# Cross-attention and quantised FFN on one core: an eight-batch loop written out, its small jobs regrouped, and maxima reduced pair by pair

## The chip, the cores and the metric

One core of a Trainium2 chip runs the whole layer for all eight batches. The metric is the device time of one execution in microseconds (us), lower is better. Times of the kernel before and after are medians of several executions.

## The reference

For each of 8 batches `x` is 512 rows by 256 and the context is 1601 rows by 256; there are 16 heads of 16 columns, all float32.

```
x   = x + attention(layernorm(x), ctx, ctx)      # 16 heads of 16, softmax over 1601 keys
h   = silu(fp4(layernorm(x)) @ fp4(Wg).T) * (fp4(layernorm(x)) @ fp4(Wu).T)
out = x + fp4(h) @ fp4(Wd).T                     # hidden width 704
fp4(v): v in blocks of 16, scaled by max|v|/6, rounded to the FP4 grid, scaled back
```

## The kernel before

**Steps.** Attention of a batch takes 52 steps: 4 groups of 4 heads, and in each group 13 tiles of the context (124 or 123 rows each, `KROWS`). A step n does this, in this order on each engine:

- TensorE (PE): `scores(n, 0)`, two score matmuls (head pair 0) into the two `st` banks; the shared jobs of side 0; `scores(n, 1)`, head pair 1 into the same two banks, each of which must first have been read by the exponential of pair 0; two "pair products" into `mx` (score rows against 512 keys, from which the softmax maximum comes); `weighted(n - 1)`, the four probability times value products of the step before into `pvb`; the shared jobs of side 1.
- ScalarE (ACT): `exps(n, 0)`, two exponentials; its share of side 0; `exps(n, 1)`; at the start of a group the copy of `pvb`; its share of side 1.
- VectorE (DVE): its share of side 0; the maxima of the step's products; its share of side 1; then the "extras" (layer norm, scales, rounding).
- GpSimd (POOL) splits queries and keys into three bf16 parts and does rounding; it has a table by step as well.

**Three batches at once.** While batch i is in attention ("att"), the same 52 steps carry the preparation of batch i + 1 ("early": context and x transposed, `q`, `k`, `v` projections) and the FFN of batch i - 1 ("late": `pvT`, `attT`, `o`, `xqT`, `gate`, `up`, `hqT`, `down`). These jobs all go through one PSUM bank, `misc`, one after the other. The dictionary `SLOTS` says which job stands in which step and on which side; each job is followed by the engine that takes its result out of `misc`. ACT takes `ctxT`, `xnT`, `q`, `k`, `v`, `attT`, `xqT`, `hqT`, `wT` and the tanh of `gate`; DVE takes `nm`, `pvT`, `o`, `gate`, `up`, `down`.

**Order of the whole.** `iterations` runs the body as pre (early work of batch 0 alone, same 52 slots), first (att of batch 0, with the FFN weights quantised and transposed, `wT`, "once"), a hardware loop `Fori(0, 6)` of six batches, last, and tail (FFN of batch 7 alone).

**Maxima.** They run 18 steps ahead of attention (`M_LEAD`). A step makes two products, one in each half of `mx`; where both are full, `maximum_of_two` reduces both (128x2048) with one DVE instruction, which frees both halves at its end.

**Queue of SyncE (SP).** It issues loads and stores in program order. In pre: context, x, then queries and keys to DRAM and back (`queries_out`, `queries_in`, `keys_out`, `keys_in`). In first, `raw_in` (FFN weights) stands right behind the next batch's context load. The context is loaded as `ctx_rows[0:123, 2:13]` from a source whose outermost dimension is those 123 rows. The projection weights come over ACT's queue at the very start.

Of the kernel before, what the change touches and what calls it, by code (L numbers as in the profile page):

```python
# [6 lines left out]
I32 = mybir.dt.int32  # L7
ALU = mybir.AluOpType
# [4 lines left out]
I = 704  # L13
NC2 = E // 128
QT = S // 128
NKT = 13
KROWS = [124, 124] + [123] * 11
# [36 lines left out]
M_LEAD = 18  # L54
BIAS_AT = STEPS - M_LEAD - 1
# [6 lines left out]

SLOTS = {
    0: ([("v", 5, "att")], []),
    1: ([("v", 6, "att")], [("pvT", 3, "late")]),
    2: ([("attT", 0, "late")], [("attT", 1, "late")]),
    3: ([("o", 0, "late")], []),
    4: ([("o", 1, "late")], []),
    5: ([("ctxT", 0, "early")], []),
    6: ([("ctxT", 1, "early")], [("ctxT", 2, "early")]),  # L70
    7: ([("ctxT", 3, "early")], [("ctxT", 4, "early")]),
    8: ([("ctxT", 5, "early")], [("nm", 1, "att")]),
    9: ([("ctxT", 6, "early")], [("xnT", 0, "early")]),
    10: ([("xnT", 1, "early")], []),
    11: ([("q", 0, "early")], [("wT", 0, "once")]),
    12: ([("k", 0, "early")], [("wT", 1, "once")]),
    13: ([("k", 1, "early")], [("wT", 2, "once")]),
    14: ([("k", 2, "early")], [("pvT", 0, "att")]),
    15: ([("k", 3, "early")], [("wT", 3, "once")]),
    17: ([("q", 1, "early")], []),  # L80
    18: ([("xqT", 0, "late")], [("xqT", 1, "late")]),
    19: ([("gate", 0, "late")], []),
    20: ([("gate", 1, "late")], [("wT", 4, "once")]),
    21: ([("k", 4, "early")], [("nm", 2, "att")]),
    22: ([("gate", 2, "late")], [("wT", 5, "once")]),
    23: ([("gate", 3, "late")], []),
    24: ([("k", 5, "early")], [("wT", 6, "once")]),
    25: ([("gate", 4, "late")], [("wT", 7, "once")]),
    26: ([("gate", 5, "late")], []),
    27: ([("k", 6, "early")], [("pvT", 1, "att")]),  # L90
    28: ([("gate", 6, "late")], []),
    29: ([("gate", 7, "late")], []),
    30: ([("k", 7, "early")], [("wT", 8, "once")]),
    31: ([("up", 0, "late")], [("wT", 9, "once")]),
    32: ([("up", 1, "late")], []),
    33: ([("up", 2, "late")], []),
    34: ([("up", 3, "late")], [("nm", 3, "att")]),
    35: ([("up", 4, "late")], [("wT", 10, "once")]),
    36: ([("up", 5, "late")], [("wT", 11, "once")]),
    37: ([("up", 6, "late")], []),  # L100
    38: ([("up", 7, "late")], []),
    39: ([("hqT", 0, "late")], [("hqT", 1, "late")]),
    40: ([("down", 0, "late")], [("pvT", 2, "att")]),
    41: ([("hqT", 2, "late")], []),
    42: ([("v", 0, "early")], [("hqT", 3, "late")]),
    43: ([("down", 1, "late")], []),
    44: ([("v", 1, "early")], [("hqT", 4, "late")]),
    45: ([("hqT", 5, "late")], []),
    46: ([("v", 2, "early")], []),
    47: ([("down", 2, "late")], [("nm", 0, "early")]),  # L110
    48: ([("v", 3, "early")], [("hqT", 6, "late")]),
    49: ([("hqT", 7, "late")], []),
    50: ([("down", 3, "late")], []),
    51: ([("v", 4, "early")], []),
# [3 lines left out]
    1: ([], [("pvT", 3, "late")]), 2: ([("attT", 0, "late")], [("attT", 1, "late")]), 3: ([("o", 0, "late"), ("o", 1, "late")], []),  # L118
# [12 lines left out]
def slots(kind, n):  # L131
    return (TAIL_SLOTS if kind == "tail" else SLOTS).get(n, ([], []))
# [3 lines left out]
for _step in SLOTS.values():  # L136
# [5 lines left out]
    1: [("early", "stats", 0)], 2: [("early", "stats", 1), ("early", "mean", 0)], 3: [("early", "root", 0)],  # L142
    4: [("early", "apply", 0)], 5: [("late", "stats", 0), ("early", "apply", 1)],
    6: [("late", "stats", 1)], 7: [("late", "mean", 0)], 9: [("late", "root", 0)],
    10: [("late", "apply", 0), ("late", "apply", 1)], 11: [("late", "xmax", 0)], 12: [("late", "xscale", 0)],
    13: [("late", "xpower", 0)], 17: [("late", "xlast", 0)],
    33: [("late", "hscale", 0)], 35: [("late", "hpower", 0)], 36: [("late", "hscale", 1)], 38: [("late", "hpower", 1)],
    39: [("late", "hscale", 2)], 41: [("late", "hpower", 2)], 42: [("late", "hscale", 3)], 44: [("late", "hpower", 3)],
}
TAIL_EXTRA = {  # L150
    5: DVE_EXTRA[5][:1], **{n: DVE_EXTRA[n] for n in (6, 7, 9, 10, 11, 12, 13, 17)},
    19: [("late", "hscale", 0)], 20: [("late", "hpower", 0), ("late", "hscale", 1)], 21: [("late", "hpower", 1), ("late", "hscale", 2)],
    22: [("late", "hpower", 2), ("late", "hscale", 3)], 23: [("late", "hpower", 3)],
}
# [12 lines left out]
class Iteration:
# [8 lines left out]
    def count(self, part, per, k):  # L176

        n = (self.ahead + SHIFT[part]) * per + k
        if isinstance(self.i, int):
            return self.i * per + n  # L180
        assert n > 0
        return self.i * per + n
# [23 lines left out]
def xattn_ffn(nc, x, ctx_in, wqT, wkT, wvT, woT, bq, bk, bv, bo, w_gate, w_up, w_down, out, scr_k, scr_q):  # L206
    es = ExitStack()
    with es:
# [58 lines left out]
        s_const, s_ones, s_w, s_x, s_x1 = (sem(n) for n in ("s_const", "s_ones", "s_w", "s_x", "s_x1"))  # L267
        s_ctx = [sem("s_ctx0"), sem("s_ctx1")]
# [15 lines left out]
        tanh_done, hs_ready, hy_ready, hm_ready, h_step, hq_ready = (sem(n) for n in ("tanh_done", "hs_ready", "hy_ready", "hm_ready", "h_step", "hq_ready"))  # L284
# [27 lines left out]
        def maxima(it, n):  # L312

            part, first = ("early", 2 * (n - STEPS + M_LEAD)) if n >= STEPS - M_LEAD else ("att", 2 * (n + M_LEAD))
            if part not in it.parts:
                return []
# [25 lines left out]
        def _(sp):  # L342
# [774 lines left out]
```

## Time and profile before

| what | value |
|---|---|
| time, median of 3 executions | 2022.91 us (2022.39 to 2029.71) |
| the profiled execution, its own time | 2027.88 us |
| its span from first to last instruction | 2026.0 us |
| busy share PE, DVE, ACT, POOL | 87%, 67%, 56%, 27% |
| mean granted TensorE clock | 0.957 |

PE is the busiest engine. Its busy time is a modelled one in which neighbouring matmuls overlap, so in this text the cost of a matmul is taken as the distance from its start to the start of what follows it. A step is measured from its first score matmul to the first score matmul of the next step. Seen so, the 2026 us are: pre 127.1, first 246.7, the six batches of the loop 226.7 to 230.5 each, last 200.8, tail 77.9. Inside first, its steps 0 to 4 take 35.2, steps 5 and 6 together 17.2, and step 19 takes 16.7; without a wait such a step is about 3.5. A loop batch without its boundary is 223.7, the same 52 steps as where straight-line code runs into the next batch.

### The profile page before, as it was taken

The numbers are of one execution on the slowest core, as the hardware profiler recorded it, in microseconds if no ns is written. First come the engines' busy times: TensorE is split into PE (matmuls) and PEld (weight loads), VectorE is DVE, ScalarE is ACT, GpSimd is POOL, SyncE is SP. The second block draws the span as 40 slices with busy tenths as digits, with TensorE's granted clock in tenths as the row PEclk, the third lists the DMA queues.
The fourth block names the chain that finished last, engine by engine and source line by source line (L and its number), as shares of the span: only waits on it lengthen the run. The fifth ranks groups of instructions, "written<-read, shape, count | busy, mean of one in ns | idle before, by whom it ended". The sixth has DMA issues, their size and how long they took to land. (4 is left out here: it accounts for less than half of the span.)

```text
span 2026.0 us, 30105 instructions
## 1 busy us (share of the span) xinstructions
PE 1754.9 (87%) x9600; PEld 730.4 (36%) x9600; DVE 1348.5 (67%) x1636; ACT 1127.0 (56%) x2239; POOL 541.8 (27%) x415
## 2 busy tenths in 40 slices
PE   3567688989999899899999899899999899989957
PEld 2222222333343334433343334433344334423425
DVE  1557576776857777676857777576867677576524
ACT  1124466666546665566546665566556665556631
POOL 3203550041320414042320514032320514000414
PEclk9677899999999999999999999999999999999988
DMA  2721431143212332134212322134212422020000
GB/s 66 154 65 27 92 72 33 54 92 65 42 39 52 78 58 40 59 74 79 46 35 52 82 58 38 61 73 71 54 32 49 89 58 39 17 33 1 6 16 11
DMA packets 97768, 109.53 MB, mean 54 GB/s; under 512 B 18484, under 2 KB 83004, under 8 KB 97596
## 3 DMA queue, kind: packets, MB, share of 16 engines
q1 hardware_dynamic: 95500, 106.21, 25.4%
q8 instruction: 89, 1.46, 0.3%
q10 hardware_dynamic: 2096, 1.18, 0.2%
q14 instruction: 83, 0.68, 0.1%
HBM read 76.78 MB, written 30.16 MB: 53 GB/s over the span
## 5 line engine op out<-in xcount | busy, mean ns | idle before, releaser
L763 ACT ACTIVATE prob<-st 123x512 f32<-123x512 f32 (+1 forms) x1664 | 906.9, 601 | 469.1 <-PE st L612 466.9
L811 DVE TENSOR_REDUCE cmx<-mx 128x4 f32<-128x2048 f32 x336 | 769.8, 2291 | 317.6 <-PE mx L626 315.9
L612 PE MATMUL st<-qstack,kstack 112*123 112x512 bf16 (+1 forms) x1664 | 554.6, 401 | 56.3 <-ACT prob L763 29.8
L641 PE MATMUL pvb<-prob,vv 123*17 123x512 f32 (+1 forms) x3328 | 446.2, 609 | 0.0
L612 PEld LDWEIGHTS st<-qstack,kstack 112*123 112x123 bf16 (+1 forms) x1664 | 201.4, 136 | 455.9 <-ACT prob L763 234.6
L626 PE MATMUL mx<-kstack,qstack 48*128 48x512 bf16 (+1 forms) x2048 | 256.6, 343 | 59.7 <-DVE cmx L811 38.1
L575 PE MATMUL misc<-wguT,rowsT 128*128 128x352 f32 x460 | 159.7, 469 | 19.1 <-DVE nmf L845 13.7
L820 DVE TENSOR_REDUCE cmx<-mx 128x2 f32<-128x1024 f32 x96 | 114.9, 1220 | 38.3 <-PE mx L626 38.2
L1021 POOL TENSOR_TENSOR cin<-cin 128x400 f32<-128x400 f32 (+1 forms) x60 | 60.8, 1013 | 284.3 <-ACT cin L716 284.2
L626 PEld LDWEIGHTS mx<-kstack,qstack 48*128 48x128 bf16 x2048 | 57.8, 95 | 216.9 <-issue 133.8
L1021 POOL TENSOR_TENSOR qx<-qx,qp 128x512 f32<-128x512 f32 x16 | 18.5, 1158 | 387.0 <-ACT qp L705 387.0
L641 PEld LDWEIGHTS pvb<-prob,vv 123*17 123x17 f32 (+1 forms) x3328 | 55.4, 95 | 159.8 <-issue 156.7
L538 PE MATMUL misc<-ctxT,wk 128*128 128x400 f32 (+1 forms) x236 | 93.2, 517 | 22.5 <-DVE att L857 12.4
L545 PE MATMUL misc<-wv,ctxT 128*123 128x256 f32 (+1 forms) x392 | 104.8, 413 | 7.1 <-DVE nmf L845 7.1
L575 PEld LDWEIGHTS misc<-wguT,rowsT 128*128 128x128 f32 x460 | 84.9, 191 | 65.8 <-DVE nmf L845 19.1
L1058 POOL TENSOR_TENSOR ht<-ht,mt 128x704 f32<-128x704 f32 x32 | 53.7, 1679 | 184.5 <-DVE mt L939 184.5
L585 PE MATMUL misc<-wdT,hqT 128*128 128x256 f32 x348 | 86.6, 390 | 4.7 <-ACT hqT L742 4.7
L1054 POOL TENSOR_TENSOR ht<-ht,rh 128x704 f32<-128x704 f32 x32 | 44.4, 1386 | 166.7 <-DVE rh L932 165.2
L545 PEld LDWEIGHTS misc<-wv,ctxT 128*123 128x123 f32 (+1 forms) x392 | 78.6, 202 | 27.3 <-DVE nmf L845 10.3
L1034 POOL TENSOR_TENSOR x<-x,bob 128x1024 f32<-128x1024 f32 x8 | 18.7, 2343 | 241.6 <-DMA x<-x 241.6
L867 DVE SCALAR_TENSOR_TENSOR ht<-hqT,misc 128x352 f32<-128x352 f32 x57 | 29.7, 521 | 75.8 <-ACT hqT L730 75.8
L585 PEld LDWEIGHTS misc<-wdT,hqT 128*128 128x128 f32 x348 | 62.4, 189 | 28.0 <-issue 10.7
(169 smaller groups left out, 1546.8 us busy)
## 6 DMA issues: line engine op xcount, KB each, us to landing
kstack<-scr_k SPq DMA_DIRECT2D x384, 100.1 KB, 4.4
scr_k<-cin SPq DMA_DIRECT2D x48, 300.0 KB, 4.3
qstack<-scr_q SPq DMA_DIRECT2D x384, 32.0 KB, 1.9
cin<-ctx_in SPq DMA_DIRECT2D x8, 1353.0 KB
scr_q<-qp SPq DMA_DIRECT2D x16, 384.0 KB, 4.2
scr_k<-cin SPq DMA_DIRECT2D x16, 300.8 KB, 4.5
xn<-x SPq DMA_DIRECT2D x8, 512.0 KB, 6.5
x<-x SPq DMA_DIRECT2D x8, 512.0 KB, 3.6
```

The costliest lines, as they stand in the source:

```text
L538: last = mm(o[:, 0:w], wk[:, h, m * 128:(m + 1) * 128], ctxT[:, h, COFF[n]:COFF[n] + w], start=(h == 0), stop=(h == NC2 - 1))
L545: last = mm(o[0:w, (kt % 2) * E:(kt % 2 + 1) * E], ctxT[:, h, KOFF[kt]:KOFF[kt] + w], wv[:, h, :], start=(kt % 2 == 0 and h == 0), stop=(h ...
L575: last = mm(o[:, 0:IH], rowsT[:, h, t * 128:(t + 1) * 128], wguT[:, h, first:first + IH], start=(h == 0), stop=(h == NC2 - 1))
L585: last = mm(o[:, 0:E], hqT[0:FW[f], f, :], wdT[0:FW[f], f, :], start=(f == 0), stop=(f == NF - 1))
L612: mm(st[0:KROWS[kt], h, :], kstack[:, hd, KOFF[kt]:KOFF[kt] + KROWS[kt]], qstack[:, hd, :], start=True, stop=True).then_inc(st_full, 1)
L626: last = mm(mx[:, q % 2, par, at:at + w], qstack[r0:r0 + LEAD, hd, t * 128:(t + 1) * 128], kstack[r0:r0 + LEAD, hd, k0:k0 + w], start=True ...
L641: last = mm(pvb[32 * h:32 * h + D + 1, :], vv[0:w, kt, HG * g + h, :], prob[0:w, n % 2, h, :], start=(kt == 0), stop=(kt == NKT - 1))
L763: activate(prob[0:KROWS[kt], n % 2, 2 * pair + h, :], st[0:KROWS[kt], h, :], ACT.Exp, scale=SCALE).then_inc(exp_done[2 * pair + h], 1)
L811: v.tensor_reduce(cmx[:, g % 2, h0:h0 + 2, at0:at1 + 1:at1 - at0], mx[:, :, :, :].rearrange("p j h n -> p h j n"), op=ALU.max, axis=AX.X). ...
L820: v.tensor_reduce(cmx[:, g % 2, h0:h0 + 2, at:at + 1], products, op=ALU.max, axis=AX.X).then_inc(max_free, 1)
L1021: g_.tensor_tensor(whole, whole, parts[:, 0, :], ALU.subtract).then_inc(step, 1)
L1058: g_.tensor_tensor(y, y, m, ALU.add).then_inc(h_step, 1)
```

## The change

- `with eng.Fori(0, B - 2)` becomes a Python `for`: the six batches are written out, and all semaphore targets become constants.
- Context tiles have 128 rows (twelve of 128, one of 65), and the context is loaded in three pieces: 2 tiles, 10 tiles, the last 65 rows.
- `SLOTS` is rewritten: the jobs that DVE takes (`nm`, `pvT`, `o`, `gate`, `up`, `down`) and `wT` stand on side 0, and most of those that ACT takes (`q`, `k`, `v`, half of `ctxT` and of `hqT`) on side 1. Some extras move by a step.
- pre has its own table: all seven `ctxT` jobs, then k 0 to 3, then `xnT` and `q`, then k 4 to 7. It does the maxima of group 0 alone (26 products, was 36); the ten others come in the first five steps of first, four products a step in place of two.
- Loads: x before the context; ACT's queue first brings only the weights and biases of `q` and `k`, the others after `ctxT`; the FFN weights (`raw_in`) move from SP's queue to ACT's, the first two pieces at the end of k 4 to 7 in pre, the later ones behind `wT` jobs.
- Tail: the rounding of x (`xround`) goes from POOL to DVE, and of the four hidden blocks DVE rounds 1 and 3 by itself (`hround`) while POOL does 0 and 2.
- `maximum_of_two` is gone: each product of a head pair has its own 128x1024 reduction, which frees its half of `mx`.

```diff
-KROWS = [124, 124] + [123] * 11
+KROWS = [128] * (T // 128) + [T % 128]
...
 SLOTS = {
-    0: ([("v", 5, "att")], []),
-    1: ([("v", 6, "att")], [("pvT", 3, "late")]),
+    0: ([], [("v", 5, "att")]),
+    1: ([("pvT", 3, "late")], [("v", 6, "att")]),
...
-    8: ([("ctxT", 5, "early")], [("nm", 1, "att")]),
-    9: ([("ctxT", 6, "early")], [("xnT", 0, "early")]),
-    10: ([("xnT", 1, "early")], []),
-    11: ([("q", 0, "early")], [("wT", 0, "once")]),
-    12: ([("k", 0, "early")], [("wT", 1, "once")]),
-    13: ([("k", 1, "early")], [("wT", 2, "once")]),
-    14: ([("k", 2, "early")], [("pvT", 0, "att")]),
-    15: ([("k", 3, "early")], [("wT", 3, "once")]),
-    17: ([("q", 1, "early")], []),
-    18: ([("xqT", 0, "late")], [("xqT", 1, "late")]),
-    19: ([("gate", 0, "late")], []),
+    8: ([("nm", 1, "att")], [("xnT", 0, "early")]),
+    9: ([("xnT", 1, "early")], [("q", 0, "early")]),
+    10: ([("wT", 0, "once")], [("k", 0, "early")]),
+    11: ([("wT", 1, "once")], [("k", 1, "early")]),
+    12: ([("wT", 2, "once")], [("k", 2, "early")]),
+    13: ([("wT", 3, "once")], [("k", 3, "early")]),
+    14: ([("pvT", 0, "att")], []),
+    15: ([], [("q", 1, "early")]),
+    17: ([("xqT", 0, "late")], [("xqT", 1, "late")]),
+    18: ([("gate", 0, "late")], []),
...
-    24: ([("k", 5, "early")], [("wT", 6, "once")]),
-    25: ([("gate", 4, "late")], [("wT", 7, "once")]),
+    24: ([("wT", 7, "once")], [("k", 5, "early")]),
+    25: ([("gate", 5, "late")], []),
...
-    50: ([("down", 3, "late")], []),
-    51: ([("v", 4, "early")], []),
+    50: ([], [("v", 3, "early")]),
+    51: ([], [("v", 4, "early")]),
 }
+PRE_SLOTS = {
+    5: ([("ctxT", j, "early") for j in range(7)], []),
+    11: ([("k", j, "early") for j in range(4)], []),
+    14: ([("xnT", j, "early") for j in range(2)], [("q", 0, "early"), ("q", 1, "early")]),
+    15: ([("k", j, "early") for j in range(4, 8)], []),
+    34: ([("v", 0, "early")], []), 36: ([("v", 1, "early")], []), 38: ([("v", 2, "early")], []), 40: ([("v", 3, "early")], []),
+    42: ([("v", 4, "early")], []), 47: ([("nm", 0, "early")], []),
+}
...
-            with eng.Fori(0, B - 2) as i:
+            for i in range(B - 2):
                 body(Iteration("loop", i, 1))
...
+            if it.kind == "first" and n < M_LATE:
+                first, number = M_GROUP + 4 * n, 4
...
-                sp.dma_start(ctx_rows[0:KROWS[0], 0:2, :], ctx_in[bi, 0:n0, :].rearrange("(t p) n -> p t n", t=2)).then_inc(s_ctx[0], 16)
-                sp.dma_start(ctx_rows[0:KROWS[2], 2:NKT, :], ctx_in[bi, n0:T, :].rearrange("(t p) n -> p t n", t=NKT - 2)).then_inc(s_ctx[1], 16)
+                for piece, (t0, t1) in enumerate(((0, 2), (2, NKT - 1))):
+                    sp.dma_start(ctx_rows[:, t0:t1, :], ctx_in[bi, t0 * 128:t1 * 128, :].rearrange("(t p) n -> p t n", p=128)).then_inc(s_ctx[piece], 16)
+                sp.dma_start(ctx_rows[0:KROWS[-1], NKT - 1, :], ctx_in[bi, n1:T, :]).then_inc(s_ctx[2], 16)
...
-                    both = maxima(it, n)
-                    if both and it.kind != "pre" and all(job[5] < M_HEADS - 1 for job in both):
-                        maximum_of_two(*both)
-                    else:
+                    todo = maxima(it, n)
+                    for both in (todo[:2], todo[2:]):
                         for job in both:
                             maximum(job)
...
+TAIL_POOL = {1: POOL_WORK[1], 19: [("late", "hscaled", 0)], 20: [("late", "hround", 0)], 21: [("late", "hscaled", 2)], 22: [("late", "hround", 2)]}
```

## Rows read from the trace of the kernel before

**Rows 1.** Windows of first and of the fourth loop batch: busy us (and instructions) of PE, PEld, DVE, ACT, POOL.

```profile
127.14:373.84 246.70, 192.50 (x1061) 65.39 (x1059) 154.65 (x153) 136.05 (x267) 77.04 (x55) 0.89 0.29 61
...
1062.40:1291.46 229.06, 211.41 (x1194) 88.82 (x1195) 163.50 (x196) 139.53 (x278) 61.85 (x49) 0.99 0.28 58
```

**Rows 2.** PE's timeline, a step with no side job (904.02) and two with (958.30, 962.02).

```profile
904.02 0.76 PE L612 MATMUL st<-qstack,kstack 112*123 112x512 bf16 x2
905.13 0.92 PE L612 MATMUL st<-qstack,kstack 112*123 112x512 bf16 x2 [0.35 <-ACT prob L763]
...
907.50 0.65 PE L612 MATMUL st<-qstack,kstack 112*123 112x512 bf16 x2
...
958.30 0.65 PE L612 MATMUL st<-qstack,kstack 112*123 112x512 bf16 x2
958.78 1.35 PE L575 MATMUL misc<-wguT,rowsT 128*128 128x352 f32 x4
959.97 0.60 PE L612 MATMUL st<-qstack,kstack 112*123 112x512 bf16 x2
...
962.02 0.65 PE L612 MATMUL st<-qstack,kstack 112*123 112x512 bf16 x2
962.50 1.51 PE L538 MATMUL misc<-ctxT,wk 128*128 128x400 f32 x4
963.85 0.60 PE L612 MATMUL st<-qstack,kstack 112*123 112x512 bf16 x2
```

**Rows 3.** ACT's timeline in the step of 962.02.

```profile
964.05 0.60 ACT L715 ACTIVATE cin<-misc,bqk 128x400 f32<-128x400 f32 x1 [0.48 <-PE misc L538]
...
965.01 1.08 ACT L763 ACTIVATE prob<-st 123x512 f32<-123x512 f32 x2
```

**Rows 4.** Groups by line: weight loads and maxima.

```profile
L811 DVE TENSOR_REDUCE cmx<-mx 128x4 f32<-128x2048 f32 x336 | 769.8, 2291 | 317.6 <-PE mx L626 315.9 <-DVE xa L920 1.1
L612 PEld LDWEIGHTS st<-qstack,kstack 112*123 112x123 bf16 (+1 forms) x1664 | 201.4, 136 | 455.9 <-ACT prob L763 234.6 <-issue 190.1
L820 DVE TENSOR_REDUCE cmx<-mx 128x2 f32<-128x1024 f32 x96 | 114.9, 1220 | 38.3 <-PE mx L626 38.2
L626 PEld LDWEIGHTS mx<-kstack,qstack 48*128 48x128 bf16 x2048 | 57.8, 95 | 216.9 <-issue 133.8 <-DVE cmx L811 48.1 <-DVE cmx L820 24.5
```

**Rows 5.** PE's timeline, where it stood idle in the fourth loop batch.

```profile
1128.86 1.61 PE L538 MATMUL misc<-ctxT,wk 128*128 128x400 f32 x4 [2.01 <-DVE att L857]
1143.07 0.66 PE L481 MATMUL misc<-ident,xa 128*128 128x128 f32 x4 [2.04 <-DVE xa L926]
1210.98 1.45 PE L575 MATMUL misc<-wguT,rowsT 128*128 128x352 f32 x4 [1.23 <-DVE nmf L845]
```

**Rows 6.** Windows: two steps over a batch boundary, into the loop and inside it.

```profile
369.58:377.98 8.40, 8.40 (x52) 4.38 (x48) 4.47 (x3) 5.45 (x12) 0.00 (x0) 1.00 0.20 67
...
827.86:841.96 14.10, 10.25 (x48) 4.86 (x46) 4.58 (x2) 6.17 (x15) 2.34 (x1) 0.88 0.39 127
```

**Rows 7.** Timeline, pre: PE after the context has landed, and the first maxima.

```profile
32.52 1.90 PE L517 MATMUL st<-ident,cin 123*128 123x123 f32 x8 [22.56 <-DMA cin<-ctx_in]
...
77.54 13.67 DVE L820 TENSOR_REDUCE cmx<-mx 128x2 f32<-128x1024 f32 x12 [5.52 <-PE mx L626]
```

**Rows 8.** Windows in the start-up: last columns are clock, share of the 16 DMA engines, GB/s.

```profile
14.00:26.00 12.00, 0.00 (x0) 0.00 (x0) 0.00 (x0) 0.00 (x0) 2.33 (x3) 1.00 0.20 67
26.00:28.00 2.00, 0.00 (x0) 0.00 (x0) 0.00 (x0) 0.00 (x0) 0.00 (x0) 1.00 0.74 210
```

**Rows 9.** Timeline in first: DVE and PE after two long waits.

```profile
149.02 1.22 DVE L957 TENSOR_REDUCE ah<-ht 88x64 f32<-88x1024 f32 x1 [13.38 <-DMA ht<-w_gate]
...
244.85 1.03 PE L626 MATMUL mx<-kstack,qstack 48*128 48x512 bf16 x4 [11.83 <-DVE cmx L811]
```

**Rows 10.** Timeline, POOL in the tail.

```profile
1990.94 1.67 POOL L1058 TENSOR_TENSOR ht<-ht,mt 128x704 f32<-128x704 f32 x1 [2.51 <-DVE mt L939]
...
2013.21 1.67 POOL L1058 TENSOR_TENSOR ht<-ht,mt 128x704 f32<-128x704 f32 x1 [1.20 <-DVE mt L939]
```

More of the change, by code:

```diff
@@ L95 @@
[L95 to L105, printed above, removed]
@@ L106 @@
-    43: ([("down", 1, "late")], []),
[L107 to L112, printed above, removed]
-    50: ([("down", 3, "late")], []),
-    51: ([("v", 4, "early")], []),
+    4: ([("o", 1, "late")], [("ctxT", 0, "early")]),
+    5: ([("ctxT", 1, "early")], [("ctxT", 2, "early")]),
+    6: ([("ctxT", 3, "early")], [("ctxT", 4, "early")]),
@@ L131, in slots @@
 def slots(kind, n):
-    return (TAIL_SLOTS if kind == "tail" else SLOTS).get(n, ([], []))
+    return {"pre": PRE_SLOTS, "tail": TAIL_SLOTS}.get(kind, SLOTS).get(n, ([], []))
 PER = {}
@@ L176, in count @@
     def count(self, part, per, k):
[L178 to L182, printed above, removed]
+        return self.batch(part) * per + k
 class SharedBanks:
@@ L312, in maxima @@
         def maxima(it, n):
-            part, first = ("early", 2 * (n - STEPS + M_LEAD)) if n >= STEPS - M_LEAD else ("att", 2 * (n + M_LEAD))
-            if part not in it.parts:
+            part, first, number = ("early", 2 * (n - STEPS + M_LEAD), 2) if n >= STEPS - M_LEAD else ("att", 2 * (n + M_LEAD), 2)
+            if it.kind == "first" and n < M_LATE:
+                first, number = M_GROUP + 4 * n, 4
+            if part not in it.parts or it.kind == "pre" and first >= M_GROUP:
                 return []
             found = []
-            for q in (first, first + 1):
+            for q in range(first, first + number):
                 g, j = divmod(q, M_GROUP)
@@ L577, in shared @@
                         t, half = divmod(j, 2)
-                        if half == 0:
+                        if half == 0 and it.kind == "tail":
+                            pe.wait_ge(hq_tail if t % 2 else hq_ready, t // 2 + 1 if t % 2 else c(QT, t // 2 + 1))
+                        elif half == 0:
                             pe.wait_ge(hq_ready, c(QT, t + 1))
@@ L653, in body @@
                         scores(n, 1)
-                    for job in maxima(it, n):
+                    products = maxima(it, n)
+                    for job in products[:2]:
                         pair_products(job)
@@ L659, in body @@
                         weighted(STEPS - 1, "late")
+                    for job in products[2:]:
+                        pair_products(job)
                     for job in jobs(it, n, 1):
@@ L776, in body @@
                         take(job)
+                        if job[0] == "wT" and job[1] in (1, 3, 5, 7):
+                            raw_in(job[1] // 2 + 2)
+                    if it.kind == "pre" and n == 5:
+                        weights_in()
+                    if it.kind == "pre" and n == 15:
+                        raw_in(0)
+                        raw_in(1)
                     if has_att:
@@ L996, in body @@
                             extra(part, what, k)
-                assert all(made[p] == LINKS[p] for p in ("early", "late") if p in it.parts), made
+                assert it.kind == "tail" or all(made[p] == LINKS[p] for p in ("early", "late") if p in it.parts), made
             iterations(dve, body)
@@ L1079, in body @@
                 for n in range(STEPS):
-                    for part, what, k in POOL_WORK.get(n, []):
+                    for part, what, k in {"pre": PRE_POOL, "tail": TAIL_POOL}.get(it.kind, POOL_WORK).get(n, []):
                         if part in it.parts:
```

199 lines of the change are left out of this document (107 added, 92 removed).

## The prediction

> **What bounds the kernel now.** I read the windows by batch first [rows 1]: a batch of the loop is 229 us with PE busy for 211, DVE for 164, ACT for 140. So the loop stands on PE, and what PE does in one step is the unit of everything below. The timeline of PE gives it [rows 2]. A full step: the first score pair takes 0.48 (958.30 to 958.78), the `gate` job 1.19 (to 959.97), and score pair 1, products and weighted matmuls the remaining 2.05 (to 962.02), 3.72 in all. Without side jobs the step is 3.48 (904.02 to 907.50), not 2.53: pair 1 starts 1.11 after pair 0 where 0.48 would do, and is stretched from 0.60 to 0.92, because both banks of `st` must first be read by the exponentials. That hole of 0.95 a step is the ACT round trip. A job on side 0 fills it; a job on side 1 does not and is paid in full. A `k` job is 1.35 (962.50 to 963.85), so on side 0 its step is 2.53 + 1.35 = 3.88.
>
> The second view is what PE waited for in a loop batch [rows 5]: the largest are 2.01, 2.04 and 1.23, the first and last because `misc` was held until DVE, busy with the 2.29 maximum, came to a side-1 `pvT` or `nm`. Adding over the 52 steps, full-use time is 209 and the batch 223.7 without its boundary; waits are thus some 15. The third is the boundary [rows 6]: two steps take 8.40 where straight-line code enters the loop and 14.10 where the loop goes back; the five returns cost 4.6 to 5.7 each, 26.6 together. The last are the waits of pre and first [rows 7 to 9].
>
> **The loop written out.** Five returns vanish: -26.6. Straight-line code ran on without a gap in the row of 8.40, so I charge nothing for fetching more of it; if fetching did cost as at a return, the term would be 0, the other bound.
>
> **Jobs by side: the term that decides.** Per batch. (a) Seventeen jobs leave side 0: 8 `k`, 2 `q`, 7 `v`. Each leaves a hole. Twelve short jobs (`pvT`, half of `ctxT` and `hqT`, about 0.49 each on PE) and four `nm` (0.12) move into or stay in holes. Counting new holes: 13 steps empty (0.95), 12 with a short job (0.46 left), four with `nm` (0.83), one of 0.7, or 21.9; the same count in the old table is 7.1. That is +14.8. (b) ACT now takes the job before the next `exps(n+1, 0)`. A `k` take is 0.96 (964.05 to 965.01) [rows 3] and starts 0.2 after the new step does, so the exponential starts at 1.16 where 0.47 would be normal: 0.7 late. An empty or short step passes this on whole; a `gate` step has slack and passes about 0.45. Four at 0.7, four at 0.45, two `q` at 0.95, five `v` that are not followed by `down` at 0.3: +8. Check of (a) and (b) on one piece: k 5 with its following `gate` is 3.88 + 3.72 = 7.60 now and would be 3.48 + 1.35 + 4.17 = 9.0. (c) Waits: `pvT` and `nm` on side 0 come before the maximum in DVE's queue, so the 2.01 and 1.23 go, with smaller ones of the kind; but `xqT` still waits about 2 for `xlast` (xround sits behind k 3 in POOL's queue, then `xlast` behind the maxima in DVE's), and in steps 32 to 38 DVE's own work (2.3 maxima, up to 2.4 `hscale`, 0.5 `up`, 1.05 `hpower`) is longer than the steps. Of 15 I keep 7: -8. Sum of (a), (b), (c): +14.8. It is bounded by +8 (ACT delays hidden) and +21 (waits not reduced).
>
> **128-row tiles.** Instruction counts stay: 13 tiles, 512 moving columns. Only the stationary width of the score matmuls changes. The row shows 136 ns for 112x123 bf16 against 95 for 48x128 bf16 [rows 4]: 41 less if it is the width. One such load per full step is exposed (the first behind `weighted`), two in a step with a hole: 27 x 0.04 + 25 x 0.08 = -3.1 per batch. Bounds: nothing, and all four per step, -8. The Trainium skill ("TensorE: Matmul & The Clock Gate", Weight-path perf modes) says that a fast weight load is used when the weights are 128 columns and not FP32; by that rule the shorter load is certain rather than likely, and the 95 ns row agrees with it. `exps`, `weighted` and `v` cost by columns and don't change.
>
> So a batch of the former loop goes from 223.7, boundary apart, to 223.7 + 14.8 - 3.1 = 235.4: +11.7, and over six batches +70, of which 26.6 comes back at the boundaries.
>
> **One reduction a pair.** Twelve in a row took 13.67 [rows 7], 1.14 each, so two are 2.28 against one of 2.29 [rows 4]. DVE's load stays and half of `mx` comes free 1.1 earlier: 0, with -0.3 per batch to +0.15 x 42 = +6 per batch as bounds if each costs its full 1.22 where DVE is behind.
>
> **Prologue.** PE got the second context piece at 32.5 after idling 22.6 [rows 7], while the DMA engines stood at 0.20 of 16 and 67 GB/s [rows 8], that is on three engines. With 128 rows the spread should be wide; at the 210 GB/s that the engines reach two microseconds later, when x joins in [rows 8], x, context and the two weights (2.7 MB) are in at about 14. The Trainium skill ("DMA: Bandwidth & Descriptors", Why a DMA increments its semaphore by 16 and not by 1) has the rule: the largest number up to 16 that divides the slowest dimension. 123 gives 3, which the 0.20 confirms, and 128 gives 16. From landing (32.5) to the first product (77) it takes 44.4 now, through `ctxT`, k 0, the splits, and SP's chain of queries and keys out to DRAM and back. The new order adds 2.5 for five loads issued on ACT's queue ahead of its take of k 0, and 2.5 because q 0, first in SP's chain, now comes after k 0 to 3: 14 + 44.4 + 5 = 63.4. Thirteen steps of two maxima, 2.28 each, with five `v` jobs at an estimated +2.3 at the lower clock (before `nm` 0 there were three): 41, to 104.4; `nm` and its rows 5.4: attention starts at 109.8, not 127.1. Taken -18; bounds -8 and -25.
>
> **First.** The wait of 13.38 for FFN weights [rows 9], behind the slow context load in SP's queue, goes, as do most of the 11.8 at step 19 (-12.5). But steps 0 to 4 now carry 20 reductions: 20 x 1.14 + norm, weight scales and powers of 12 make 35 on DVE, where the five took 35.2 with the wait in it; steps 5 and 6 (17.2) fall to 9. Moved `k`, `q`, `v` cost +5.5 here. Sum -15; bounds -3 and -25.
>
> **Last, tail.** Last: `pvT` in holes (4 x 0.49), loads -4, bank waits -2, v +2: -6. Tail: POOL's four roundings start 7.4 apart, 1990.9 to 2013.2 [rows 10]; two of them go to DVE, which at the same time is stretched by POOL's; I count -4.5, and -2.5 for xround, -7 (bounds 0 and -12).
>
> **Sum.** 70 - 26.6 - 18 - 15 - 6 - 7 = -2.6 against the profiled execution's 2027.9: 2025.3. That execution was 5 above the median of the runs, 2022.9, so the same difference gives 2020.3. I forecast 2020: no change that can be measured.
>
> **Rivals.**
> - *The holes are cheaper than counted* (faster). If ACT's delays vanish in slack and most waits go, the side term is +8 per batch: 6 x (14.8 - 8) = 41 less, 1979. For it: 15 us of waits existed and many are of the kind that is attacked. Against: `exps` are strictly behind the take in ACT's queue. It decides from +12 per batch down. Chance 0.32.
> - *Behind every side-1 job ACT runs late* (slower). The side term is +20 per batch because in steps 10 to 13 the `k` takes of ACT, the splits of POOL and the exponentials form one chain, and DVE in 32 to 38 adds its wait: +31, 2051. For it: four such steps follow each other with nothing on side 0. Against: steps with two ACT copies now stretch only by 0.1 to 0.3. It decides from +17.5. Chance 0.24.
> - *The written-out loop fetches as slowly as a return*: +26.6 and so 2047; against it the row of 8.40. It is within the slower case, a quarter of it.
> - The forecast case, holes and waits about as counted: 0.44, of which 0.09 falls below -0.5% and 0.07 above.
>
> Half a per cent (10 us) is about what a measurement of this kernel tells from no change. Faster: 0.32 + 0.09 = 0.41. Slower: 0.24 + 0.07 = 0.31. Same: 0.28. The range of 8 in 10 takes in both rivals' times: 1975 to 2055; the likeliest case's own is 2003 to 2037.
>
> **What would show it.** In the profile after: batches of equal length near 235 with no gap at their boundary; 3.48 to 3.54 in empty steps less 0.08; steps 10 to 13 at 5.5 each; `gate` steps after a `k` at 4.17 and others at 3.68; the score weight load at 95 ns; the context load landed by 14 to 16 and attention starting near 110; first near 232 with steps 0 to 4 at 7 each on DVE; a tail near 71. A batch below 231 or above 239 makes the forecast wrong, since each us of it counts six times; so would a start of attention after 120.

## The result, and the profile after

The changed kernel takes 2091.18 us (median of 4, 2087.65 to 2093.01) against 2023.93 for the kernel before on the same chip: ratio 1.0325, 95% interval 1.03 to 1.035. It is 3% slower. The forecast was 2020, no change that can be measured, with a range of 1975 to 2055: the result lies 36 above the range.

| stage | before | after | change | forecast |
|---|---|---|---|---|
| pre | 127.1 | 102.9 | -24.2 | -18 |
| first | 246.7 | 248.0 | +1.3 | -15 |
| six middle batches | 1373.5 | 1467.2 | +93.7 | +43.4 |
| last | 200.8 | 194.9 | -5.9 | -6 |
| tail | 77.9 | 78.0 | +0.1 | -7 |
| span | 2026.0 | 2091.1 | +65.1 | -2.6 |

The windows of first and of the fourth middle batch answer to [rows 1].

```profile
102.90:350.90 248.00, 199.11 (x1078) 60.47 (x1079) 174.13 (x205) 134.45 (x265) 77.16 (x55) 0.93 0.31 66
1085.50:1330.10 244.60, 217.70 (x1195) 81.00 (x1194) 163.17 (x240) 139.89 (x278) 60.37 (x49) 0.99 0.26 54
```

PE's instruction count (1195 against 1194) and the busy times of DVE and ACT are those of before, and yet the batch is 15.5 longer. PE's modelled busy time grew by 6.3 with the same instructions (its clock fell in two steps of this batch, and neighbouring matmuls overlap less); the rest is idle time. So the loss is no work added; it is order. PE's timeline shows where, here in the third middle batch: in k 4's step and the `gate` step behind it (941.78, 946.87), and in k 5's step, with nothing on side 0 and k on side 1 (955.22); it answers to [rows 2].

```profile
941.78 0.60 PE L601 MATMUL st<-qstack,kstack 112*128 112x512 bf16 x2
...
945.41 1.61 PE L524 MATMUL misc<-ctxT,wk 128*128 128x401 f32 x4
946.87 0.59 PE L601 MATMUL st<-qstack,kstack 112*128 112x512 bf16 x2
948.20 1.45 PE L562 MATMUL misc<-wguT,rowsT 128*128 128x352 f32 x4 [0.74 <-ACT cin L722]
949.49 0.60 PE L601 MATMUL st<-qstack,kstack 112*128 112x512 bf16 x2
...
955.22 0.60 PE L601 MATMUL st<-qstack,kstack 112*128 112x512 bf16 x2
956.36 0.88 PE L601 MATMUL st<-qstack,kstack 112*128 112x512 bf16 x2 [0.54 <-ACT prob L769]
957.17 0.61 PE L615 MATMUL mx<-kstack,qstack 48*128 48x512 bf16 x4
957.71 1.05 PE L630 MATMUL pvb<-prob,vv 128*17 128x512 f32 x8
958.69 1.61 PE L524 MATMUL misc<-ctxT,wk 128*128 128x400 f32 x4
960.14 0.60 PE L601 MATMUL st<-qstack,kstack 112*65 112x512 bf16 x2
```

The step of 955.22 takes 4.92. Its second score pair comes 1.14 after the first with nothing in between: the hole. Then k is paid in full, 1.45. The step of 946.87 takes 4.67 (next pair 0 at 951.54), where a plain `gate` step is 3.68. Two things stretch it, and both hang on ACT, whose timeline answers to [rows 3].

```profile
947.07 0.59 ACT L721 ACTIVATE cin<-misc,bqk 128x401 f32<-128x401 f32 x1 [2.20 <-PE misc L524]
947.56 0.59 ACT L722 ACTIVATE cin<-misc,bqk 128x401 bf16<-128x401 f32 x1
948.04 1.08 ACT L769 ACTIVATE prob<-st 128x512 f32<-128x512 f32 x2
```

The exponential of the new step starts at 948.04, 1.17 after the score pair where 0.48 is normal (a plain `gate` step, 964.82 to 965.30). And the `misc` bank is held until L722 has read it, so `gate` starts at 1.33 instead of 0.44 and its 1.29 ends at 949.49, behind the exponential and not inside its time.

What was forecast right is seen too. Two groups by line answer to [rows 4]: the score weight load is 99 ns where it was 136, and the large maxima are all single.

```profile
L601 PEld LDWEIGHTS st<-qstack,kstack 112*128 112x128 bf16 (+1 forms) x1664 | 145.2, 99 | 534.7 <-ACT prob L769 325.6
L827 DVE TENSOR_REDUCE cmx<-mx 128x2 f32<-128x1024 f32 x768 | 905.2, 1218 | 329.4 <-PE mx L615 328.1
```

At the batch boundary of 840.17 (the timeline of PE) the last `v` job of one batch runs into the first score pair of the next; the two steps around it take 5.56 and 5.57, where a return of the loop made them 13.11 to 14.20 (the pair in [rows 6] is 14.06). In the start-up windows the DMA engines stand at 0.95 and 275 GB/s, against 0.20 and 67 [rows 8], and PE starts on the large context piece at 12.01.

```profile
838.34 1.99 PE L532 MATMUL misc<-wv,ctxT 128*128 128x256 f32 x8
840.17 0.60 PE L601 MATMUL st<-qstack,kstack 112*128 112x512 bf16 x2
...
6.00:12.00 6.00, 1.08 (x4) 0.71 (x4) 5.73 (x10) 0.74 (x2) 6.00 (x1) 1.00 0.95 275
```

### The profile page after: what moved, and what is told of

It is laid out like the page before. It is cut to its first block, busy times and chain, and to the rows that moved or that the text cites. A ratio compares the mean times of both kernels' runs of the same rounds, so it can differ in the third digit from the quotient of the medians.

```text
span 2091.1 us, 26267 instructions
## 1 busy us (share of the span) xinstructions
PE 1783.9 (85%) x9600; PEld 667.5 (32%) x9600; DVE 1371.0 (66%) x1982; ACT 1127.8 (54%) x2239; POOL 518.2 (25%) x405
## 4 chain that ended last, share of the span: by engine, by line
PE 62%; ACT 17%; DVE 14%; issue 4%; DMA 1%; SPq 1%; POOL 0%; ACTq 0%; DVEq 0%
PE pvb L630 17%; ACT prob L769 11%; PE st L601 11%; PE mx L615 9%; DVE cmx L827 8%; PE misc L562 6%; PE misc L532 5%; PE misc L524 4%; PE misc L574 4%; ACT cin L722 2%; PE misc L512 1%; PE misc L550 1%; ACT vv L727 1%; PE misc L465 1%; DVE cmx L829 1%
## 5 line engine op out<-in xcount | busy, mean ns | idle before, releaser
L827 DVE TENSOR_REDUCE cmx<-mx 128x2 f32<-128x1024 f32 x768 | 905.2, 1218 | 329.4 <-PE mx L615 328.1
L769 ACT ACTIVATE prob<-st 128x512 f32<-128x512 f32 (+1 forms) x1664 | 905.2, 600 | 363.3 <-PE st L601 362.3
L601 PE MATMUL st<-qstack,kstack 112*128 112x512 bf16 (+1 forms) x1664 | 548.3, 389 | 125.4 <-ACT prob L769 99.1
L630 PE MATMUL pvb<-prob,vv 128*17 128x512 f32 (+1 forms) x3328 | 447.2, 610 | 0.0
L601 PEld LDWEIGHTS st<-qstack,kstack 112*128 112x128 bf16 (+1 forms) x1664 | 145.2, 99 | 534.7 <-ACT prob L769 325.6
L562 PE MATMUL misc<-wguT,rowsT 128*128 128x352 f32 x460 | 160.7, 472 | 24.1 <-ACT cin L722 17.8
L721 ACT ACTIVATE cin<-misc,bqk 128x400 f32<-128x400 f32 (+1 forms) x59 | 35.2, 596 | 143.4 <-PE misc L524 129.4
L630 PEld LDWEIGHTS pvb<-prob,vv 128*17 128x17 f32 (+1 forms) x3328 | 55.4, 95 | 158.1 <-issue 151.6
L727 ACT COPY vv<-misc 128x256 f32<-128x256 f32 (+1 forms) x96 | 31.4, 375 | 136.6 <-PE misc L532 136.6
L532 PE MATMUL misc<-wv,ctxT 128*128 128x256 f32 (+1 forms) x384 | 99.7, 402 | 0.0
L532 PEld LDWEIGHTS misc<-wv,ctxT 128*128 128x128 f32 (+1 forms) x384 | 69.2, 191 | 51.4 <-issue 42.6
```

The costliest lines, as they stand in the source:

```text
L532: last = mm(o[0:w, (kt % 2) * E:(kt % 2 + 1) * E], ctxT[:, h, KOFF[kt]:KOFF[kt] + w], wv[:, h, :], start=(kt % 2 == 0 and h == 0), stop=(h ...
L562: last = mm(o[:, 0:IH], rowsT[:, h, t * 128:(t + 1) * 128], wguT[:, h, first:first + IH], start=(h == 0), stop=(h == NC2 - 1))
L601: mm(st[0:KROWS[kt], h, :], kstack[:, hd, KOFF[kt]:KOFF[kt] + KROWS[kt]], qstack[:, hd, :], start=True, stop=True).then_inc(st_full, 1)
L630: last = mm(pvb[32 * h:32 * h + D + 1, :], vv[0:w, kt, HG * g + h, :], prob[0:w, n % 2, h, :], start=(kt == 0), stop=(kt == NKT - 1))
L727: last = copy(vv[0:w, kt, :, 0:D], src[0:w, (kt % 2) * E:(kt % 2 + 1) * E].rearrange("p (h d) -> p h d", h=H))
L769: activate(prob[0:KROWS[kt], n % 2, 2 * pair + h, :], st[0:KROWS[kt], h, :], ACT.Exp, scale=SCALE).then_inc(exp_done[2 * pair + h], 1)
```

## Experiments

Each ran beside the kernel before, whose median was 2021.3 to 2022.9 there; ratios are to it. "Changed" is the changed kernel, 2091, which was not run again beside them. Steps and batches are read from the profiled execution of each run. The diffs show the lines that matter; `...` stands for the others.

**1. The old placement in the changed kernel.** `SLOTS` and the step tables of the extras and of POOL's work as before, everything else changed.

```diff
-    10: ([("wT", 0, "once")], [("k", 0, "early")]),
+    10: ([("xnT", 1, "early")], []),
...
-    24: ([("wT", 7, "once")], [("k", 5, "early")]),
-    25: ([("gate", 5, "late")], []),
+    24: ([("k", 5, "early")], [("wT", 6, "once")]),
+    25: ([("gate", 4, "late")], [("wT", 7, "once")]),
```

> The changed kernel with the job tables of the kernel before (SLOTS and the step numbers of the extras and of GpSimd's work), everything else as changed. Theory 'placement': the changed kernel's loop batches are 244.6 us where 223.7 plus nothing for boundaries was possible; k, q and v on side 1 leave the hole, delay the exponentials and hold the misc bank. Then a loop batch here is 219 to 224 us and the whole 1930 to 1960 us. Rival 'reduction': the split maxima made the batches longer; then a batch stays above 238 us and the whole above 2050. Rival 'code or tiles': written-out code or 128-row tiles cost it; the same, above 2050.

1944.79, ratio 0.962 (0.9601 to 0.9639). The middle batches take 222.6 to 224.2, the fourth in this window:

```profile
999.10:1223.00 223.90, 210.35 (x1198) 81.62 (x1194) 166.25 (x241) 139.49 (x278) 62.18 (x50) 0.98 0.28 59
```

Placement alone costs 146: 21.4 in each middle batch (244.5 against 223.1 on average) and 19.3 in first (248.0 against 228.7). All else that was changed is a gain of 77. Falls of the clock are not the difference: with every step taken at its shortest of the six middle batches, a batch is 242.9 against 220.9, 22.0 apart.

**2. One reduction for two again.** In the changed kernel, `maximum_of_two` is back.

```diff
...
+                        if both and it.kind != "pre" and all(job[5] < M_HEADS - 1 for job in both):
+                            maximum_of_two(*both)
+                            continue
                         for job in both:
                             maximum(job)
```

> The changed kernel with one 128x2048 reduction for both products of a step again, where both are full. Theory 'placement': twelve 128x1024 reductions in a row took 13.67 us, 1.14 each, so two cost what one of 2.29 does, and the whole stays within 10 us of 2091. Rival 'reduction': the whole falls by 30 us or more.

2105.56, ratio 1.0418 (1.0394 to 1.0443): 14 slower, of it 6 in first, 3 in last, about 1 in a middle batch.

**3. Only the loop written out**, in the kernel before (with it, its semaphore targets become constants).

```diff
-            with eng.Fori(0, B - 2) as i:
+            for i in range(B - 2):
```

> The kernel before with its six-batch loop written out and nothing else. Theory: the five returns of the loop cost 26.6 us in the profile and go, 1995 to 2000 us. Rival 'code': fetching straight-line code is as slow as a return, then 2023 or more.

1997.05, ratio 0.9886 (0.9862 to 0.9911): -24, where the term was -26.6. The two steps around each boundary take 4.26 each, 8.52 together, exactly as where first runs into the loop in the kernel before: no cost of straight-line code is seen there.

**4. Only the tiles**, in the kernel before: `KROWS` and the three-piece load.

```diff
-KROWS = [124, 124] + [123] * 11
+KROWS = [128] * (T // 128) + [T % 128]
```

> The kernel before with 128-row context tiles and the context loaded in three pieces, nothing else. Theory: the score weight load falls from 136 to 99 ns, which is worth 2 to 4 us a batch (15 to 30 in all), and the context of batch 0 lands some 18 us earlier, and the FFN weights behind it in the queue, some 12 to 20 more: 1960 to 1990 us, with steps without a job 3.40 to 3.48 and full gate steps 3.68. Rival: the loads of weights are hidden and the start-up is bound elsewhere: 2015 to 2023.

1982.95, ratio 0.9805 (0.9776 to 0.9833): -38, most of it the load (attention starts at 106.1, step 3 of first takes 3.86 and not 18.54). In the middle batches most steps are 0.04 shorter; step by step, each at its shortest of six, that is 1.4 a batch.

**5. Six of the eight k jobs on side 0**, in the changed kernel, the others left as a control. One of six such lines; `wT` jobs, which exist in first alone, go to side 1 in exchange.

```diff
...
-    24: ([("wT", 7, "once")], [("k", 5, "early")]),
+    24: ([("k", 5, "early")], [("wT", 7, "once")]),
```

> The changed kernel with six of its eight k jobs on side 0 again: k 0 to 3 (steps 10 to 13) and k 5 and 7 (steps 24 and 30); k 4 and 6 stay on side 1 as a control in the same batch. Theory (a job on side 1 fills no hole, and ACT's exponentials run late behind its take): a k step falls from 4.92 to 3.84, the gate step behind it from 4.67 to 3.68, steps 10 to 13 from 23 to 25 together to about 17.5; 2 x 2.07 + 6.5 = 10.6 less in each loop batch, steps 21, 22, 27 and 28 unchanged, total near 2018. Rival (the side is innocent, the moved extras, POOL's splits or a lower clock stretch these steps): the six steps keep 4.92 and 5.6, the total stays above 2080.

2018.86, ratio 0.9985 (0.9975 to 0.9995): 72 of the 146. Steps 24 and 25 take 3.84 and 3.73 (were 4.92 and 4.67), the control steps 27 and 28 stay at 4.96 and 4.67 in the same batch. PE's timeline of steps 24 (918.04) and 25 (921.87):

```profile
918.04 0.60 PE L601 MATMUL st<-qstack,kstack 112*128 112x512 bf16 x2
918.48 1.51 PE L524 MATMUL misc<-ctxT,wk 128*128 128x400 f32 x4
919.83 0.60 PE L601 MATMUL st<-qstack,kstack 112*128 112x512 bf16 x2
...
921.87 0.66 PE L601 MATMUL st<-qstack,kstack 112*65 112x512 bf16 x2
...
925.61 0.61 PE L601 MATMUL st<-qstack,kstack 112*128 112x512 bf16 x2
```

**6. Five of the seven v jobs on side 0**, in the changed kernel; one of five such lines.

```diff
...
-    42: ([], [("v", 0, "early")]),
+    42: ([("v", 0, "early")], []),
```

> The changed kernel with five of its seven v jobs (v 0, 1, 3, 4, 5) on side 0 again, v 2 and v 6 left on side 1. Theory: steps 42, 44, 50, 51 and 0 fall from 5.30 to 5.57 each to 4.2 to 4.7, the steps behind them by 0.2 to 0.3 where they hold a short job; about 5.5 less in each loop batch, near 2050 in all. Rival (v on PE is so short that only ACT's two copies count, and these stand before an exponential on either side): less than 2 a batch, above 2075.

2042.9, ratio 1.0101 (1.0083 to 1.0118): 48 of the 146. Steps 42 and 44 fall from 5.30 to 4.22, `down` behind the first from 5.94 to 5.39, and step 51 from 5.56 to 4.24: a batch is 7.0 shorter, more than the 5.5 expected. Runs 5 and 6 move nothing but the side of eleven jobs and give 120 of the 146 if they add up. The other 26 (the other `k` and `v`, `q`, the moved extras) were not taken apart.

**7. Only the split reduction**, in the kernel before.

```diff
-                    if both and it.kind != "pre" and all(job[5] < M_HEADS - 1 for job in both):
-                        maximum_of_two(*both)
-                    else:
-                        for job in both:
-                            maximum(job)
+                    for job in both:
+                        maximum(job)
```

> The kernel before with one change: each product of a pair has its own reduction, nothing else. The prediction gave this step zero. Undone in the changed kernel it cost 14 (6 in first, 3 in last, about 1 in a loop batch). If that is a property of the step, the kernel before gains as much: waits of PE for the 2.29 maximum in steps 15, 18, 22, 40, 47 get shorter by up to 1.1 each, 10 to 25 in all. Rival (it only pays beside the four products a step in first and beside DVE jobs on side 0): within 5 of before.

2013.94, ratio 0.9953 (0.9934 to 0.9971): -8, a real but smaller gain than expected. It sits where DVE has a side-1 job, in that step or the one behind: step 15 from 6.10 to 5.15, step 14 from 4.84 to 4.32, and 0.22 in each of steps 9, 22 and 48, behind an `nm`.

**8. Old placement, pvT 0 in the empty step, DVE's tail rounding last.** The diff is against run 1.

```diff
-    14: ([("k", 2, "early")], [("pvT", 0, "att")]),
+    14: ([("k", 2, "early")], []),
+    16: ([("pvT", 0, "att")], []),
```

> The changed kernel with the old placement (1945 in the earlier run) and two repairs. pvT 0, which DVE takes, goes from side 1 of step 14 to side 0 of the empty step 16: step 14 from 4.67 to 3.84, step 15 from 7.80 to 3.84, step 16 from 3.47 to 4.06, so 4.2 less in each of seven batches. In the tail DVE rounds hidden blocks 1 and 3 behind its gate and up jobs and not between them: PE's wait of 3.2 and ACT's of 8.7 go, the last rounding ends 4 to 5 earlier. Total near 1910 to 1915. Rival (PE then waits for something else just behind, xqT at step 18 or the exponentials): less than 2 a batch, above 1930.

1925.36, ratio 0.9532 (0.9515 to 0.955). Step 15 falls from 7.80 (6.23 in one batch) to 3.90, and step 16, which now holds `pvT` 0 in its hole, stays at 3.47; batches are 3.7 shorter. The tail grew from 76.8 to 80.0: block 1, now rounded last, came when PE had waited 7.77 for it.

**9. nm ahead on side 0, weight rounding of first later, another tail order.** Three edits in separate stages; the diff is against run 8.

```diff
-    34: ([("up", 3, "late")], [("nm", 3, "att")]),
-    35: ([("up", 4, "late")], [("wT", 10, "once")]),
+    34: ([("up", 3, "late")], []),
+    35: ([("nm", 3, "att"), ("up", 4, "late")], [("wT", 10, "once")]),
...
-W_SCALE_AT = {1: 0, 4: 1, 14: 2, 17: 3, 25: 4, 29: 5}
+W_SCALE_AT = {5: 0, 8: 1, 14: 2, 17: 3, 25: 4, 29: 5}
```

> The kernel of the last run (old placement, pvT 0 at step 16, 1925) with three more edits that act in different stages. (1) Each nm, which DVE takes, goes from side 1 of its step to the front of side 0 of the next one: steps 22, 35 and 48 stood at 4.73, 5.27 and 5.76 since the job behind waited for DVE to come to nm behind its maxima; expected 0.3 + 0.8 + 1.0 less, 2 in a batch. Rival: DVE is still in the maxima of the step before, the job behind nm on the same side waits just as long, nothing gained. (2) In first the scales and powers of weight pieces 0 and 1 move from steps 1 to 6 to steps 5 to 10: DVE's 4-element norm operations took 2.1 to 2.3 each while POOL rounded weights in steps 3 and 4; step 4 falls from 13.65 to about 6, first by 5 to 8. Rival: the 20 reductions set these steps, nothing gained. (3) In the tail DVE rounds block 1 before the scale of block 3 and the power of block 2. The tail was 80.0 with rounding behind everything, and PE then needs 4.7 a block from block 1 on; expected 75.5. Total near 1900 to 1905.

1921.2, ratio 0.9502 (0.9488 to 0.9516). (1) missed: steps 34 and 35 went from 3.79 and 5.27 to 3.68 and 5.38. DVE comes when its maxima are done, wherever the job stands. (2) half: step 4 fell from 13.65 to 6.56, but steps 7 and 9 gave most of it back (4.07 to 6.38, 4.11 to 9.17); first is 4 shorter. (3) the tail missed by 2: 77.6.

**10. A longer take.** In the changed kernel ACT copies k 5 and k 7 a third time (an extra copy that no result needs).

```diff
+                        if j in (5, 7):
+                            act.wait_ge(k_split[1], c(4, j - 4))
+                            activate(kx[0][:, 0:w], src[:, 0:w], ACT.Identity, bias=bqk[:, 1, m:m + 1]).then_inc(s_twice, 1)
```

> The changed kernel with a third copy of 400 columns in ACT's take of k 5 and k 7 (both on side 1, steps 24 and 30), ahead of the two that are there; k 4 and k 6 are the control. If the step behind a side-1 k is long because ACT's exponentials start behind the take, steps 25 and 31 grow from 4.67 by one copy, 0.5 (and in first, where they hold no gate, from 4.15 to 4.6), while steps 24 and 30 stay at 4.92. If it is long because of PE's own order, nothing moves. About 1 per batch, 2099 in all.

2099.84, ratio 1.038 (1.0362 to 1.0397). Steps 24 and 30 stay at 4.92; 25 and 31 grow from 4.67 to 5.16; in first, step 25 without a `gate` from 4.15 to 4.63. PE's timeline of step 25:

```profile
961.14 0.60 PE L602 MATMUL st<-qstack,kstack 112*65 112x512 bf16 x2
962.97 1.45 PE L563 MATMUL misc<-wguT,rowsT 128*128 128x352 f32 x4 [1.23 <-ACT cin L728]
964.25 0.60 PE L602 MATMUL st<-qstack,kstack 112*65 112x512 bf16 x2
```

PE's wait for the bank is 1.23 where it was 0.74. The whole copy, 0.49, arrives in the step's length, with a `gate` or without: there is no slack. The control step 28 keeps its 4.67.

**11. The hole filled.** Useless matmuls on side 0, one in step 24, two in step 30 of each middle batch.

```diff
+                    if it.kind == "loop" and n in (24, 30):
+                        before = ("gate", 4, "late") if n == 24 else ("up", 0, "late")
+                        pe.wait_ge(free[before[0]], job_count(it, before))
+                        filler(misc, 1 if n == 24 else 2)
```

> The changed kernel with useless matmuls (128x352 f32, results overwritten) on side 0 of two loop steps whose k job stands on side 1: one in step 24, two in step 30, as much as a gate job. If a side-1 job leaves a hole of 0.95 on side 0, one matmul (0.6) is free and step 24 stays at 4.92, two (1.19) add 0.2 to 0.3, step 30 at 5.2. If there is no hole and PE's work simply adds up, the steps are 5.5 and 6.1. Total 2092 to 2094 by the first, 2102 by the second.

2096.67, ratio 1.0362 (1.0343 to 1.0381). Step 24 stays at 4.92, step 30 is 5.13. PE's timeline of step 24 (its end is 959.87):

```profile
954.95 0.60 PE L605 MATMUL st<-qstack,kstack 112*128 112x512 bf16 x2
955.39 0.76 PE L589 MATMUL misc<-wguT,rowsT 128*128 128x352 f32 x2
956.09 0.88 PE L605 MATMUL st<-qstack,kstack 112*128 112x512 bf16 x2
```

Pair 1 comes 1.14 after pair 0, exactly as without the filler: 0.6 of PE's work was free. The second filler of step 30 cost 0.21. Of the 5.5 in the total (4.4 between the two profiles) the fillers explain 1.3; the rest is in places far from them, 1.5 in a fall of the clock in step 17 of last and 1.7 in the tail.

**12. xlast one step earlier**, with both weight scales of first together and the changed kernel's tail order. The diff is against run 9.

```diff
-    13: [("late", "xpower", 0)], 17: [("late", "xlast", 0)],
+    13: [("late", "xpower", 0)], 16: [("late", "xlast", 0)],
```

> The kernel of the last but one edit set (1921) with three more. (1) xlast, DVE's last rounding operation of x, goes from step 17 to step 16. There POOL had finished at 834.8, DVE stood idle for 1.86, and xlast at 840.3, behind the maxima of step 17, made PE wait 2.16 for xqT in step 18; behind that wait the step took 6.00, 7.1 or 8.6, the longer ones with a fallen clock. If the wait brings the fall on, step 18 goes to 4.2 in every batch, about 3 less on average, 18 in all. Rival (the fall comes anyway): 1.8 less, 11 in all. (2) In first both weight scales stand in steps 5 and 6, ahead of POOL's first rounding, whose neighbourhood stretched DVE's small operations: steps 7 and 9 (6.38 and 9.17) fall by 5 together; rival: PE then waits for the powers, nothing. (3) The tail has the changed kernel's order again, 76.8 against 77.6. Total 1893 to 1905.

1896.77, ratio 0.9384 (0.9369 to 0.9399), the fastest version. All six middle batches take 216.1 to 216.4, step 18 is 3.96 in each. So (1) gave 17.8 in the middle batches and 3.2 in last, the case in which the wait brings the fall of the clock on. (2) missed: step 9 fell by 4.8, steps 10 and 11 grew by 5.0. (3) the tail is 77.3. The windows of step 18, of run 9 and of this one:

```profile
1057.23:1065.81 8.58, 6.37 (x28) 2.33 (x25) 5.21 (x5) 3.05 (x6) 3.71 (x3) 0.64 0.78 134
```

```profile
1046.85:1050.81 3.96, 3.81 (x28) 1.58 (x25) 2.85 (x4) 2.94 (x6) 2.85 (x3) 1.00 0.31 103
```

## Why the prediction was wrong

**The failed step is "Jobs by side", +14.8 a batch.** It measured 21.4 (run 1); 6.6 too little, six times, is 40 of the 68 by which the sum missed. The mechanism was right: the hole exists (run 11), the side-1 job is paid in full, ACT runs late behind it (run 10). The sizes were not:

- In (a), a job that leaves side 0 was charged the hole, 0.95. In its own step a `k` costs 1.08 more on side 1 (4.92 against 3.84, run 5), and so does a `v` (5.30 against 4.22, run 6). If that holds for all seventeen jobs, the 0.13 above the charge is 2.2 a batch; `q` was not measured alone.
- In (b), "a gate step has slack and passes about 0.45". It has none. The `gate` step behind a k grew by 0.94 (4.67 against 3.73, run 5), 0.49 above the charge and 2.0 a batch for the four of them. Of the 0.94, 0.68 is ACT's lateness, which shows alone in first (4.15 against 3.47 in a step without `gate`), and 0.26 comes because the one `misc` bank is held until the take ends, and `gate` then ends behind the exponential. The argument forgot that the job behind needs the same bank. The piece checked in advance, 7.60 to 9.0, was 7.57 (run 5; 7.71 in the kernel before) to 9.59.
- Also in (b), a `down` behind a `v` was charged nothing and paid 0.55 (5.94 against 5.39, run 6).
- In (c), `pvT` 0's wait of 2.01 went, and `xqT` waited 1.94, both as said. But the `nm` jobs still waited for DVE, 0.47 to 1.34 each, and step 34, which holds only one of them, took 4.11 where an empty step is 3.47. What remains of the 6.6, some 2, was not taken apart.

The second rival ("behind every side-1 job ACT runs late", +20, decided from +17.5) was this case, held for 0.24. Its place was right in part: of the 21.4, steps 10 to 13 carry 7.8 (23.6 against 15.8 in run 1), but steps 19 to 31, with k 4 to 7 and the `gate` steps behind them, carry 5.7. And it varied one term with all else at its forecast, so it stopped at 2051, and the range with it.

**A batch without the side term** was put at 220.6 and is 223.1 (run 1): 15 in six batches. With every step at its shortest it is 220.9; the other 2.2 are falls of the clock behind the waits of steps 15 and 18 (below), which the sum had at nothing. That 220.6 was met so closely is partly luck: the tiles gave 1.4 a batch and not 3.1 (run 4), and the split maxima, put at 0, made up for about 1.0 of it (run 1 against run 3, less the tiles' 1.4). Of the 55 so far, 5 are offset: 1373.5 less six times 223.7 is 31.3, where the sum took 26.6 for the returns, since the batches before had falls of the clock too (step 15 took 7.79 in the first middle batch, 6.10 in others).

**First**, -15, was +1.3. Here too it is placement: +19.3 measured for "+5.5". With the old placement first was 18 shorter than before. Steps 0 to 4 were forecast at 35 and took 40.5; 4.1 of it is two small operations of DVE that waited out POOL's (below).

**Tail**, -7, was 0. `xround` on DVE gave its 2.3. `hround` 1 on DVE stands ahead of the `gate` and `up` of the next step; three orders gave 76.8 and 77.3, 80.0, and 77.6 (runs 1 and 12, 8, 9), none more than 1.1 below the 77.9 of before. Which order is best these runs don't tell: the changed kernel's own order gave 76.8 to 80.3 over runs 1, 2, 5, 6 and 10 to 12, with a granted clock of 0.85 to 0.79. The timeline of PE after shows the cost, and that here the low clock follows the wait (2.71, where four such matmuls take 1.35):

```profile
2064.36 2.71 PE L562 MATMUL st<-wguT,rowsT 128*128 128x352 f32 x4 [3.20 <-DVE ht L874]
```

**One reduction a pair**, "0, with -0.3 per batch" as bound, was a gain of 8 in the kernel before (run 7; step by step, each at its shortest of six, 2.4 a middle batch) and 14 in the changed one (run 2, 6 of it in first with its four products a step). DVE's load stays, as said; but the first reduction needs only the first product, and DVE is sooner at the job behind. That is argued from the steps where the gain sits, not measured by itself.

**Right:** the loop written out (-24 for -26.6; the prediction's 8.40 for the two steps of entry stops 0.12 early, they take 8.52, and 26.6 is the sum by that number), the score weight load (99 ns for 95, though its worth was half of that forecast), and last (-5.9 for -6). Last was partly luck: its step 17 took 5.55, and 7.09 in run 11, where the clock fell in it. **Pre** was better than forecast, -24.2: the context landed by 12, not 14 to 16, the first product came at 59.8, not 63.4, and attention started at 102.9. The Trainium skill ("DMA: Bandwidth & Descriptors", Why a DMA increments its semaphore by 16 and not by 1) has the rule that 128 divides among 16; the 0.95 of the windows agrees.

## What to carry to other kernels

Where a bank is read by one engine and written by another in turn, the writer has a hole in each step; fill it with the longest jobs that another engine doesn't delay, and before moving a job out, count the hole, the reader's lateness and whatever shares the job's bank, each whole. Test a placement one job at a time against a control in the same batch. When a rival raises one term, ask what it does to the other stages: the same mistake was made in the six batches and in first.

## What the runs showed of the hardware

**A wait of PE of about 2 us can lower its clock, and then costs more than itself.** In run 9 step 18 held the same wait of 2.16 in each middle batch, and took 6.00 in three, 7.57 and 7.58 in two and 8.58 in one; in the window above the granted clock is 0.64, between the two levels, 2.4 GHz (1.00) and 1.2 GHz (0.50). The eight `weighted` matmuls took 1.91 there, against 1.05. Without the wait (run 12) the clock is 1.00 and the step 3.96 in every batch. Step 15 of run 1 is a second case: behind a wait of 2.13 it took 7.80 to 7.86 in five batches (clock 0.78) and 6.23 in one (1.00), and 3.90 in all once the wait was gone (run 8). In the changed kernel falls also stand behind shorter waits, though no run took these away: after 1.41 for the exponential step 10 took 7.44 (clock 0.77) in the third middle batch and 5.79 in most, after 1.22 step 13 took 6.91 (0.81) in the fourth and 5.60 in most. That it comes only sometimes behind the same wait (8.58 in the fourth middle batch of run 9, 6.00 in the third) is seen; what decides it is open.

**DVE's smallest operations waited for POOL's.** The timeline of DVE in first of the changed kernel, and that of POOL:

```profile
134.99 2.11 DVE L906 TENSOR_SCALAR ve<-mv 128x4 f32<-128x4 f32 x1
137.14 0.17 DVE L907 TENSOR_SCALAR hv<-ve 128x4 f32<-128x4 f32 x1
137.21 2.31 DVE L908 TENSOR_SCALAR rs<-ve 128x4 int32<-128x4 int32 x1
```

```profile
134.74 2.33 POOL L1096 TENSOR_TENSOR ht<-ht,mt 88x1024 f32<-88x1024 f32 x1 [10.90 <-DVE mt L992]
137.15 2.35 POOL L1098 TENSOR_TENSOR ht<-ht,mt 88x1024 f32<-88x1024 f32 x1
```

Operations on four elements a partition take 2.11 and 2.31, where such a one takes 0.17 alone, ending within 0.03 of the end of the POOL operation beside them (137.07, 139.50), and 0.17 between. At the very start the first of them took 4.33, ending 0.03 behind POOL's first large memset. The Trainium skill ("SBUF — State Buffer", SBUF: two separate sides) describes the port pair that both share as an exclusive lock, held for the whole instruction by whichever starts first, and names the DVE operations that take it: those in a mode with two ports or with two SBUF inputs. The trace agrees in that DVE's operation ends with POOL's. So POOL's long operations are better kept away from chains of small ones on DVE, but in runs 9 and 12 the time only moved to other steps of first.
